# First attention: TensorE's instructions in another order, with the row maxima joined on TensorE and VectorE

## The reference

```python
q = z @ wq @ fcq_w + fcq_b        # z = layernorm(x); 16 heads of 64
k = z @ wk @ fck_w + fck_b
v = z @ wv @ fcv_w + fcv_b
scores = jnp.einsum('bihd,bjhd->bhij', q, k) / scale
attn = jax.nn.softmax(scores, axis=-1)
out = jnp.einsum('bhij,bjhd->bihd', attn, v)
out = out.reshape(b, n, N_HEAD * D_V)
return out @ fco_w + fco_b
```

## Time and profile before

| | us |
|---|---|
| median of 3 runs (1483.03 to 1488.1) | 1483.71 |
| time of the profiled execution | 1486.37 |
| its span in the trace | 1484.6 |
| busy: TensorE / VectorE / GpSimd / ScalarE | 1381.6 / 999.2 / 863.1 / 817.5 |
| first score tile of the stage, last values | 63.84, 744.92 |

### The profile page before, as it was taken

The page is one execution under the profiler, slowest core; times in us unless marked ns, Lnnn a source line. Parts: engine busy times, 40 slices in busy tenths (PEclk is TensorE's granted clock), DMA queues, the critical chain, the costliest instruction groups (busy, mean ns, idle before and its releaser), DMA issues. The chain is left out here.

```text
span 1484.6 us, 18636 instructions
## 1 busy us (share of the span) xinstructions
PE 1381.6 (93%) x6322; PEld 783.4 (53%) x6322; DVE 999.2 (67%) x1675; ACT 817.5 (55%) x1236; POOL 863.1 (58%) x685
## 2 busy tenths in 40 slices
PE   6699999999999999999978977899999997999998
PEld 5344444444444444544456734454444445787776
DVE  5676777777677777677666678676666725566665
ACT  4244444444444445444545443566776565787776
POOL 0298777777977777787744505455565332344443
PEclk9699999999999999999999997999999998999999
DMA  3110111111011111000050005012111106000000
GB/s 107 33 44 16 58 59 44 58 58 48 26 58 58 51 52 44 15 16 15 26 159 1 1 0 100 15 24 30 21 30 29 30 2 271 1 1 8 8 8 8
DMA packets 32586, 60.59 MB, mean 41 GB/s; under 512 B 9499, under 2 KB 17084, under 8 KB 32348
## 3 DMA queue, kind: packets, MB, share of 16 engines
q1 hardware_dynamic: 32492, 59.40, 14.4%
HBM read 35.13 MB, written 13.89 MB: 33 GB/s over the span
## 5 line engine op out<-in xcount | busy, mean ns | idle before, releaser
L628 POOL TENSOR_TENSOR psum_k<-psum_k,prob 128x1024 f32<-128x1024 f32 x186 | 457.9, 2485 | 46.5 <-ACT prob L680 46.5
L680 ACT ACTIVATE prob<-pair 128x1024 f32<-128x1024 f32 x256 | 250.5, 1025 | 378.7 <-PE pair L932 378.7
L738 DVE TENSOR_REDUCE mx<-pair 128x2 f32<-128x1024 f32 x256 | 305.3, 1222 | 100.0 <-PE pair L865 99.5
L904 PE MATMUL pv<-prob,c_all 128*64 128x512 f32 x1024 | 247.9, 605 | 0.0
L1935 DVE CUSTOM_DVE_ANT_0 l_banks<-l_banks,causal 128x128 f32<-128x128 f32 (+7 forms) x256 | 189.5, 782 | 75.8 <-PE l_banks L1973 74.7
L931 PE MATMUL pair<-qq,ak 128*128 128x512 f32 x512 | 221.5, 433 | 7.1 <-DVE q L732 3.3
L1843 ACT ACTIVATE l_prob<-l_banks 128x1024 f32<-128x1024 f32 (+7 forms) x256 | 155.3, 654 | 111.7 <-PE l_banks L1992 111.0
L932 PE MATMUL pair<-q,kb 128*128 128x512 f32 x512 | 202.4, 395 | 0.0
L2151 POOL TENSOR_TENSOR silu_rest_t<-silu_t,silu_lead_t 128x512 fp32r<-128x512 f32 x74 | 96.4, 1304 | 145.0 <-ACT silu_lead_t L2348 145.0
L1897 POOL TENSOR_SCALAR_AFFINE_SELECT l_prob<-l_prob 128x128 f32<-128x128 f32 x256 | 72.3, 295 | 146.9 <-ACT l_prob L1843 145.3
L623 POOL TENSOR_TENSOR psum_k<-prob 128x1024 f32<-128x1024 f32 x31 | 74.1, 2412 | 118.9 <-ACT prob L680 118.9
(11 more groups left out here) (318 smaller groups left out, 2276.8 us busy)
## 6 DMA issues: line engine op xcount, KB each, us to landing
plain<-scratch_sums SPq DMA_DIRECT2D x32, 256.0 KB
whole<-in_experts SPq DMA_DIRECT2D x12, 512.0 KB, 5.1
scratch_lead<-rounded SPq DMA_DIRECT2D x12, 512.0 KB, 2.6
scratch_rest<-rounded SPq DMA_DIRECT2D x12, 512.0 KB, 3.9
w_lead_t<-scratch_lead SPq DMA_DIRECT2D x9, 512.0 KB, 6.6
w_rest_t<-scratch_rest SPq DMA_DIRECT2D x9, 512.0 KB, 7.4
l_kk<-rounded SPq DMA_DIRECT2D x16, 256.0 KB, 4.2
l_qq<-rounded SPq DMA_DIRECT2D x16, 256.0 KB, 5.4
```

Source lines behind the costliest of these rows:

```text
L628: nc.gpsimd.tensor_tensor(total[:, h, :], total[:, h, :], prob[kt % 4][:, h, :], ALU.add).then_inc(summed, 1)
L680: nc.scalar.activation(prob[kt % 4][:, :, ts(j, BLK)], buffer("ST", at)[:, :, :], ACT.Exp, scale=D0 ** -0.5).then_inc(exp_done, 1)
L738: nc.vector.reduce_max(mx[:, x % 2, :, x // 2], buf[:, :, :], AX.X).then_inc(read, 1)
L904: ins = nc.tensor.matmul(pv[D0 * h:D0 * (h + 1), ts(j, BLK)], m.c_all[:, TT * (s // PAIRS) + kt, :], prob[kt % 4][:, h, ts(j, BLK)], start ...
```

## The change

The two tables become one list, `STEP`, of kinds, and for the last step `LAST_STEP`. The n-th ST of the list is score tile n (key tile n // 2, half n % 2); the n-th PV is half n - 4 (`VALUES_BEHIND`), so that the first four PV of a step are the last four halves of the step before, and the last four of the whole stage come behind its script. A step now has the scores in groups of 3, 1, 4, 4, 2 and 2 tiles, and m, g, R and P stand ahead of the last two. The two rows of maxima in `mx` are not joined by VectorE in SBUF before m: m transposes both, and VectorE takes the maximum of the two out of PSUM (`top`, back into PSUM) before `mrow`. SyncE issues the transfer of the shift row (`shift_rows`) ahead of that of the maxima. Some small ScalarE parts of steps 12 to 15 are placed by score tile numbers (TURN_AT and so on).

```diff
-AFTER_SCORES = {
-    0: [("q", 0), ("q", 1)],
...
+STEP = ("ST ST ST q q ST PV PV s s s PV PV ST ST ST ST l s s PV PV X r s s s n PV PV ST ST ST ST PV "
+        "PV s s s PV PV PV s s s PV PV s s PV ST ST m g R P ST ST ").split()
+LAST_STEP = ("ST ST ST ST PV PV PV PV ST ST ST ST l PV PV PV PV ST ST ST ST PV PV r PV PV ST ST ST ST n "
+             "PV PV PV PV g ").split()
+VALUES_BEHIND = 4
+TURN_AT, ROOT_AT, NORMAL_AT, LEAD_AT, EXP_AT = 7, 11, (3, 7), 11, 3
...
-    for kt in range(TT):
-        out += [("ST", kt, 0), ("ST", kt, 1)]
-        out += [("UNIT",) + u for u in AFTER_SCORES.get(kt, []) if u in has]
-        if kt or n:
-            out += [("PV", kt - 1, 0), ("PV", kt - 1, 1)]
-        out += [("UNIT",) + u for u in AFTER_VALUES.get(kt, []) if u in has]
+    for kind in STEP if n + 1 < STEPS0 else LAST_STEP:
+        x = at[kind]
+        at[kind] += 1
+        if kind in ("ST", "PV"):
+            if x >= 0 or n:
+                out.append((kind, x // 2, x % 2))
+        elif (kind, x) in has:
+            out.append(("UNIT", kind, x))
...
                 if n + 1 < STEPS0:
+                    shift_rows(n + 1)
                     max_rows(n + 1, place(n, ("m", 0)))
-                    shift_rows(n + 1)
...
-                    if x == S_UNITS - 1:
-
-                        v.wait_ge(read, u + 1)
-                        nc.vector.tensor_tensor(mmax[:, :, :], mx[:, 0, :, :], mx[:, 1, :, :], ALU.max
-                                                ).then_inc(mmax_ready, 1)
...
-                    nc.vector.scalar_tensor_tensor(mrow[:, :], buf[0:2 * TT, 0, 0:P], -1.0, tcol[:, :],
+                    top = buf[0:2 * TT, 1, 0:P]
+                    nc.vector.reduce_max(top, buf[0:2 * TT, 0, 0:2 * P].rearrange("p (a n) -> p n a", a=2), AX.X
+                                         ).then_inc(top_ready, 1)
+                    v.wait_ge(top_ready, k + 1)
+                    nc.vector.scalar_tensor_tensor(mrow[:, :], top, -1.0, tcol[:, :],
...
-                    pe.wait_ge(mmax_ready, k + 1)
-                    ins = nc.tensor.matmul(buf[0:2 * TT, 0, 0:P], mmax[:, :, :].rearrange("p h t -> p (h t)"),
-                                           m.ident[:, :], start=True, stop=True)
+                    pe.wait_ge(read, place(k - 1, ("s", S_UNITS - 1)) + 1)
+                    for half in R2:
+                        ins = nc.tensor.matmul(buf[0:2 * TT, 0, ts(half, P)],
+                                               mx[:, half, :, :].rearrange("p h t -> p (h t)"), m.ident[:, :],
+                                               start=True, stop=True)
...
-            for j in R2:
-                product(STEPS0 - 1, TT - 1, j)
+            for x in range(2 * TT - VALUES_BEHIND, 2 * TT):
+                product(LAST, x // 2, x % 2)
```

More of the change, by code:

```diff
@@ L1 @@
 import numpy as np
+from collections import defaultdict
 from contextlib import ExitStack
@@ L465, in l0_attention @@
         mx = sb("mx", [P, 2, 2, TT])
-        mmax = sb("mmax", [P, 2, TT])
         tcol = sb("tcol", [2 * TT, P])
@@ L666, in _ @@
                         kt, j = rest
-                        if kt < 0:
+                        if kt == -1:
                             keep_product(n - 1, j)
@@ L683, in _ @@
                             lead_piece(piece_of(n), kt - 4)
-                        if j and kt == 2 and n == AT_TURN:
+                        if 2 * kt + j == TURN_AT and n == AT_TURN:
                             act.wait_ge(read, place(PAIRS, ("g", 0)) + 1)
@@ L693, in _ @@
                                                  ).then_inc(early_act, 1)
-                        if j and kt < 2 and n == AT_LOGITS:
+                        if 2 * kt + j in NORMAL_AT and n == AT_LOGITS:
                             act.wait_ge(early_dve, CENTRE)
                             act.wait_ge(read, place(AT_TURN, ("R", 0)) + 1)
-                            for t in range(TPB * kt, TPB * (kt + 1)):
+                            part = NORMAL_AT.index(2 * kt + j)
+                            for t in range(TPB * part, TPB * (part + 1)):
                                 ins = nc.scalar.activation(normal[:, t, :], m.x[:, t, :], ACT.Identity,
```

16 lines of the change are left out of this document (5 added, 11 removed).

## The result

| | before | after |
|---|---|---|
| median of 14 runs each, us | 1485.88 | 1477.39 |
| lowest and highest, us | 1482.87, 1488.47 | 1473.78, 1482.9 |
| profiled execution, its span, us | 1486.37, 1484.6 | 1481.03, 1479.3 |
| mean granted clock of TensorE in it | 0.972 | 0.963 |

The ratio of the times is 0.9946, interval 0.9932 to 0.9961: the change gains 8.0 us, about the 0.5% that can be told from nothing. The forecast was 1468.2, with 1479 as its upper end: the sign was right, the gain about half of what was predicted. Between the two profiled executions 5.3 us went, where the sum said 15.5; the profiled execution of the changed kernel is one of its slower ones, 3.6 above the median. The times now spread over 9 us where they spread over 6.

A forecast was written before the change was run, and what follows sets the result against it. TensorE was taken to set the pace of the first attention stage. 13 full steps gave -19.2, first two steps -0.3, last stretch +4.0: total -15.5 us, a predicted median of 1468.2 us, range 1458 to 1479.

The forecast's parts named there:

- TensorE's own time: TensorE's runs per step: scores -0.81, s -0.55, m +0.24, together -1.12 us per step.
- Rival D: Order changes but transitions cost the same, part of the spacing being weight loading; 1486 us; chance 0.05.
- rival A: VectorE finds GpSimd idle at L812 and the tail's g waits little; 1460 us; chance 0.13.
- The wait behind q: TensorE waits 0.45 us at the second s, where waits were 0.81 per step; change -0.36 per step.
- `on` (L775) now stands ... 0.7 us of cover: VectorE before the last eight s: on ends at 13.0 us after l, 0.7 us of cover until m, costed at nothing.
- Rival C: on waits for reciprocals before the last eight maxima; each us beyond 0.7 costs 1 us x 13; 1491 at 8.7; chance 0.05.
- m to the next step's first scores ... cover 0.6: Step's seam: row of maxima lands at 3.2 us, TensorE is busy till 3.8; costed at nothing.
- First two steps ... -0.3: Stage start: s and scores wait on VectorE and ScalarE as before, longer way of m +0.5; together -0.3 us.
- Last stretch: +4.0: From the last m on: -1.5 TensorE groups, +3.7 and +1.8 for waits at g, P and l's copy; +4.0 us.
- rival B: Covers of tenths of a us fail, taking 0.3 to 1.2 us from each of 13 steps; 1478 at 0.8; chance 0.17.

The follow-up runs named there:

- experiment 3: e3_sums: changed kernel with l ahead of the second group of four score tiles and r right behind them; median 1469.14 us, ratio 0.9872 to the kernel before.
- experiment 9: e9_fetch: changed kernel with 32 tiny matmuls between the first s units, shifting the instruction packets; one execution, 1471.03 us.
- experiment 10: Changed kernel with 16 tiny matmuls between the first s units, shifting the instruction packets; one execution, 1475.47 us.
- experiment 8: e8_shift_late: changed kernel with the shift row's transfer issued behind that of the maxima again; median 1479.1 us, ratio 0.9953 to the kernel before.
- experiment 6: e6_order_only: changed kernel with mmax made by VectorE in SBUF again and m transposing once; median 1466.15 us, ratio 0.9851 to the kernel before.
- experiment 7: Kernel before with only the new form of m (both rows transposed, maximum out of PSUM); median 1489.96 us, ratio 1.0023 to the kernel before.
- experiment 11: e10_best: changed kernel with earlier last-step n, old-alternation first step, earlier sums and statistics, mmax joined in SBUF; median 1456.76 us, ratio 0.9788 to the kernel before.
- e1_tail: experiment 1: changed kernel with n (on) between the last two pairs of score tiles in the last step; median 1474.95 us, ratio 0.9903 to the kernel before.
- experiment 4: Changed kernel with step 13's layernorm statistics behind the third and eighth maximum, not fourth and ninth; median 1476.86 us, ratio 0.9935 to the kernel before.
- e11_no_first: As experiment 11, but with the first step in the changed kernel's order; median 1459.01 us, ratio 0.9799 to the kernel before.

## Why the prediction was right or wrong, point by point

**TensorE's own time: right, a little low.** The prices of going in and coming out held for scores (3.88 for 3.9). The s were better: four groups of three take 1.16, 1.05, 0.89 and 1.24, together 4.34, with 0.78 of waits in them, against 4.12 + 0.45, and the two groups of two 0.67 for 0.70. Rival D is refuted: a tile in a long run costs 0.23 per matmul, with a change of form about 0.1 at the borders of scores and hardly any from s to values. The ten regular steps gave 1.82 and not 1.48. At 41.20 they lie beside the 41.1 that the prediction gave as a sign of rival A.

**The wait behind q: right** in place, 0.27 for 0.45.

**"`on` (L775) now stands ... 0.7 us of cover": a step that failed.** The end of `on` was right (13.15 behind l, 13.0 predicted). But the cover was reckoned at m alone, the end of the eight maxima. Between, the ring lets TensorE run ahead of them by three s only, and there nothing was left: 0.35 of wait in every full step (experiment 3), and a later `on` is passed on in full. The term also missed that the store's landing has a second value, 2.7 to 3.4, and that the lock makes the price a step: nothing more up to 7.5 behind the store, 2.3 from 7.6 on. Rival C had the mechanism, and its sign, idle time before `on` that ends at a DMA, is in every full step. It was priced as 1 us for each us beyond the cover in 13 steps; it is 2.3 in none, one or two steps per execution (two here, with a fall of the clock behind one). Experiments 3, 9 and 10 show both halves: with the sums early no step is long, and with the packets elsewhere another step is.

**"m to the next step's first scores ... cover 0.6": right for full steps (experiment 8), wrong for the form of m as a whole.** Its price on TensorE was in the sum as 0.24 (0.22 measured). What wasn't is that VectorE's own chain is longer by 0.66, and through L812 and q this comes back to TensorE: 0.25 more in this order (experiment 6), nothing in the old one (experiment 7), and nothing with the sums early (experiment 11). As 0.45 of wait for q stood in the sum, the total of a step doesn't suffer by it.

**"First two steps ... -0.3": the step that missed most**, +4.5 in the distances. What it counted was right: without falls and without a late row the first distance is 39.05 (e1_tail, e8_shift_late) and the second 40.16 (e9_fetch), 0.6 less than before. It put at nothing a late landing of the row of maxima and the clock. The row's landing at 3.04 cost 1.3 (a wait of 1.89 for 0.63; experiment 9 takes it away), the two falls 1.6 each, and 0.6 is left for the lower level's 7.3 us behind the first row instead of 5.0. Together 5.1, less the 0.6. All five falls begin within 0.8 us of the end of a wait, so the waits may have to do with it. They don't decide it: e1_tail, e3_sums, e6_order_only and e8_shift_late have the same three waits in the first step (0.48, 0.84, 0.53) and no fall there. What decides stays open.

**"Last stretch: +4.0": right in its mechanism** (3.63 for 3.8, and experiment 1 takes it away). Without the clock the stretch would have cost 3.3; the fall of 734.1 is 1.6 more, and 0.6 lies behind the stage.

**Not in the sum at all:** the statistics of distance 14, 2.5 us (experiment 4). They stood behind the fourth and the ninth maximum before as well, when VectorE had slack there (43.47 for 43.03); the new order brings the s in threes, and VectorE is then behind.

Taken together, the profile misses the sum by 10.2. By the prices above, the clock is 6.9 of it (two falls and the longer start, 3.8; 1.5 in distance 15; 1.6 at the end), late landings 5.9 (the row 1.3, two stores 2.3 each), the statistics 2.5; the steps, the first row and the ends were otherwise better than the sum and give some 5 back. The forecast also stood on a median before of 1483.71 from three runs, where fourteen have 1485.88. That 1477.39 is close to the 1478 of rival B is luck: B had tenths of a us failing in each of 13 steps, and the full steps came out better than forecast.

## What to carry to other kernels

When an operation that waits for a DMA is put ahead of other work in an in-order queue, ask for a cover that holds its late landing too, and not only the median of the trace: here 1.4 was usual and about 3 came once or twice per execution. Reckon such a cover at every place where the buffers let the other engine wait, and not only at the end of the row. Where two operations shut each other out as `on` and GpSimd's additions do here, a delay is paid in whole operations of the other engine. A new order must be walked through at its ends apart, where neighbours are missing and the clock may fall; a sum of full steps says nothing about them. And when two kernels are compared by one execution each, first see which of the difference is falls of the clock and late landings: here they moved up to 8.4 us, as much as the whole gain.

## What the runs showed of the hardware

- A packet of the instruction queue (16 KB, 0.9 to 1.4 us long, one about every 28 us) that started 0.70 to 1.16 behind the issue of an 8 KB store moved its read-back from 1.4 to between 2.7 and 3.4 us behind the issue, in 13 of 13 cases. At 1.23 and 1.31 behind (e11_no_first, e10_best, distance 14) it didn't.
- The row of maxima, 8 KB, lands 1.8 behind its issue (about 2.4 in the kernels that send the shift row behind it), and 3.04 to 3.55 where such a packet starts 0.96 to 1.49 behind it.
- `on` (two SBUF operands) beside GpSimd's additions ended 8.74 to 8.77 behind the store's issue (8.87 in distance 14) for starts of 5.8 to 7.5, and 11.07 to 11.09 for starts of 7.6 to 8.3; a small `mmax` takes 0.18 or 1.58.
- A third s in a row starts 0.23 behind the second, which starts 0.33 behind the first.
- The clock fell for 3.4 us at a time (once 6.8, in e9_fetch), up to four times in this stage and once just behind it, at a price of 1.6 us in a group of scores; the same waits came with a fall in some executions and without one in others.
